# Two expert stages of a four-layer block: normalisation of batches 0 to 6 placed inside the attentions ahead, pairs turned early, gates and first products moved

## The reference, cut to what matters

```python
mod = (_silu(L1_c) @ L1_wmod).reshape(L1_c.shape[0], 6, 1, -1)
sa, ca, ga, sb, cb, gb = (mod[:, 0], mod[:, 1], mod[:, 2], mod[:, 3], mod[:, 4], mod[:, 5])
...
gb = (2 * (gb >= 0) - 1) * jnp.maximum(jnp.abs(gb), 0.25)
...
x = x + ga * _L1_attn_ref(h, ...)
h = _layernorm(x, axis=-1) * (1 + cb) + sb
x = x + gb * _L1_ffn_ref(h, ...)          # top 4 of 32 experts by router logits, and a shared one
```

```python
a = entmax15(layernorm_noaffine(jnp.einsum('btd,de->bte', x, proj)))
g1 = jnp.einsum('bte,er->btr', a, C1)
z = jnp.einsum('btd,dr->btr', xb, Win) * gate     # first product of cp_mumoe
```

## Time and profile before

| | us |
|---|---|
| median of 3 runs | 2562.01 |
| lowest and highest of them | 2559.89, 2563.37 |
| the profiled execution | 2557.01 |
| its span in the trace | 2555.2 |
| layer 1: from the last DVE step of the attention to the logits | 1299.4 to 1344.1 |
| layer 2: from the last row maximum to the first expert product | 1896.9 to 1968.1 |

### The profile page before, as it was taken

How to read it: one execution, slowest core, us unless ns; L and a number is a source line. 1 busy time by engine, 2 the same in 40 slices (tenths; PEclk the granted TensorE clock), 3 DMA queues, 4 the chain that set the end, 5 groups by cost and what they waited for, 6 DMA issues and landing times.

```text
span 2555.2 us, 44079 instructions
## 1 busy us (share of the span) xinstructions
PE 1982.7 (78%) x14690; PEld 1390.1 (54%) x14690; DVE 1679.9 (66%) x5339; ACT 1151.9 (45%) x3371; POOL 894.7 (35%) x1178
## 2 busy tenths in 40 slices
PE   5888889963377667765589999995875799999955
PEld 3545666651266556554575666663443466666642
DVE  6776453245778887888757766665745466666547
ACT  2533333418677777777422222221442355555520
POOL 4433121033456745764440000003410155555511
PEclk7977989975555555555559999996995899999967
DMA  3111000020000000000010000002101000000000
GB/s 124 48 40 40 14 24 27 2 86 23 7 13 7 14 7 14 7 7 1 1 47 1 1 0 0 0 0 46 48 28 63 12 1 1 1 1 1 1 1 17
DMA packets 57812, 49.62 MB, mean 19 GB/s; under 512 B 7049, under 2 KB 55913, under 8 KB 57065
## 3 DMA queue, kind: packets, MB, share of 16 engines
q1 hardware_dynamic: 54548, 45.53, 5.6%
q10 hardware_dynamic: 3040, 1.38, 0.2%
HBM read 19.78 MB, written 1.05 MB: 8 GB/s over the span
## 4 chain that ended last, share of the span: by engine, by line
PE 41%; DVE 28%; SPq 9%; ACT 8%; issue 8%; POOL 5%; DMA 1%; ACTq 0%; DVEq 0%; POOLq 0%
SPq L570 8%; PE bank L1565 5%; PE bank L1557 4%; PE bank L1558 4%; DVE weights L2572 4%; PE bank L1282 3%; PE bank L1634 3%; ACT rope_c L3431 3%; ACT rope_s L3431 3%; PE bank L1671 3%; PE bank L1298 3%; PE bank L1683 2%; DVE small L2610 2%; POOL big L721 2%; DVE feat_o L2622 2%
## 5 line engine op out<-in xcount | busy, mean ns | idle before, releaser
L1468 PE MATMUL bank<-V,probsT 128*128 128x9 f32 x1024 | 236.2, 364 | 76.6 <-ACT probsT L3442 76.6
L1468 PEld LDWEIGHTS bank<-V,probsT 128*128 128x128 f32 x1024 | 226.3, 329 | 114.0 <-ACT probsT L3442 94.4
L2212 DVE TENSOR_REDUCE nmax<-bank 128x4 f32<-128x1024 f32 x144 | 176.0, 1222 | 88.1 <-PE bank L1095 87.9
L3497 ACT ACTIVATE hid<-bank 128x512 f32<-128x512 f32 x144 | 85.6, 597 | 278.1 <-PE bank L1558 268.3
L1565 PEld LDWEIGHTS bank<-weights,hid 128*128 128x128 f32 x1152 | 149.9, 191 | 76.0 <-issue 65.2
L2812 DVE TENSOR_TENSOR hid<-hid,bank 128x512 f32<-128x512 f32 x144 | 98.6, 687 | 117.0 <-PE bank L1565 113.7
L1565 PE MATMUL bank<-weights,hid 128*128 128x128 f32 x1152 | 151.9, 275 | 8.9 <-DVE O L2826 5.1
L3442 ACT ACTIVATE probsT<-bank 128x512 f32<-128x512 f32 x128 | 76.0, 597 | 179.8 <-PE bank L1455 177.4
L1557 PE MATMUL bank<-O,weights 128*128 128x512 f32 x288 | 149.2, 600 | 0.0
L1558 PE MATMUL bank<-O,weights 128*128 128x512 f32 x288 | 147.9, 595 | 0.0
L815 POOL MEMSET big<- 128x4096 bf16 x1 | 3.5, 3511 | 403.6 <-DVE x L2852 403.6
(11 more groups left out here) (664 smaller groups left out, 5502.5 us busy)
## 6 DMA issues: line engine op xcount, KB each, us to landing
qT<-parts SPq DMA_DIRECT2D x276, 32.0 KB
big<-V SPq DMA_DIRECT2D x192, 32.0 KB
big<-parts SPq DMA_DIRECT2D x180, 32.0 KB
weights<-in_weights_l_ffn SPq DMA_DIRECT2D x1, 4832.0 KB, 15.1
weights<-in_weights_l_attn SPq DMA_DIRECT2D x1, 3904.0 KB, 12.6
weights<-in_weights_l_ffn SPq DMA_DIRECT2D x1, 3628.0 KB, 14.3
qT<-V SPq DMA_DIRECT2D x96, 32.0 KB
weights<-in_weights_l_ffn SPq DMA_DIRECT2D x1, 2304.0 KB, 7.9
```

The lines of the kernel that those rows point to most:

```text
L1468: last = mm(pb[1][:, t * S + h * wide:t * S + (h + 1) * wide], probsT[:, h % 2, at:at + P], values_of(b, k)[:, h * wide:(h + 1) * wide], s ...
L2212: V_.tensor_reduce(to, scored.rearrange("p (i a n) -> p i a n", i=HPG, n=n), AX.X, ALU.max, negate=True).then_inc(score_max.sem, 1)
```

## The change

Statistics and normalisation are cut in three groups: batches 0 to 5 (12 tiles), batch 6 (2 tiles), batch 7 (2 tiles), as `FRONT_GROUPS`. Groups 0 and 1 are done inside the attention ahead, group 2 in the front. New helpers `wide_stats_of`, `wide_norm_of` (DVE) and `wide_root` (POOL) do one group each.

```diff
+        FRONT_GROUPS = ((0, B - 2), (B - 2, B - 1), (B - 1, B))
...
+            def wide_root(ph, g):
+                (first, end), (_, _, var_w, rstd_w) = FRONT_GROUPS[g], front_room(ph)
+                at = slice(T * first, T * end)
+                pool.wait_ge(wide_var_ready.sem, wide_var_ready(ph, 0, g + 1))
+                nc.gpsimd.tensor_tensor(rstd_w[:, at], var_w[:, at], minus_half[:, at], ALU.pow).then_inc(wide_rstd_ready.sem, 1)
...
                 for m, there in iterations(ph):
+                    if m in (3 * B - 1, 3 * B):
+                        wide_root("l2_ffn", m - 3 * B + 1)
                     if there(0):
                         split_max(m, 1)
...
+                wide_root("l1_ffn", 0)
+                wide_root("l1_ffn", 1)
                 add_out(B - 1)
...
             def wide_front(ph, logits):
-                pe.wait_ge(pass_done.sem, pass_done(ph, 0, 1))
...
+                for u in range(PAIRS - 1):
+                    turn(u)
                 pe.wait_ge(wide_silu.sem, wide_silu(ph, 0, 1))
                 for b in range(B):
                     last = mm(pb[6 + b // 4][:, b % 4 * D:(b % 4 + 1) * D], silu_8[:, b, :], W(ph, "wmod")[:, 2 * D:3 * D],
                               start=True, stop=True)
                 last.then_inc(wide_mod.sem, 1)
...
+                for u in range(PAIRS - 1):
+                    logits_of(u)
+                turn(PAIRS - 1)
+                logits_of(PAIRS - 1)
...
                 wide_front(ph, "proj")
+                for u in range(PAIRS):
+                    if u == 0:
+                        pe.wait_ge(wide_var_ready.sem, wide_var_ready(ph, 0, 4))
+                    if u == 2:
+                        pe.wait_ge(delta_ready, 1)
+                    mm(pb[RANK_BANKS[u]][0:R2, :], W(ph, "win1"), feats[:, 2 * u:2 * u + 2, :].rearrange("p r k -> p (r k)"),
+                       start=True, stop=True).then_inc(z_psum.sem, 1)
                 pe.wait_ge(mix_ready, 1)
...
                 for m, there in iterations(ph):
                     for k in range(NU):
+                        if m in (3 * B - 1, 3 * B) and k in (0, 3):
+                            (wide_norm_of if k else wide_stats_of)("l2_ffn", m - 3 * B + 1)
...
+                wide_stats_of("l1_ffn", 0)
+                wide_stats_of("l1_ffn", 1)
+                wide_norm_of("l1_ffn", 0)
+                wide_norm_of("l1_ffn", 1)
                 weighed(B - 1)
                 l1_result(B - 1)
...
                 logits = pb[1][:, 0:N16 * E2].rearrange("p (j e) -> p j e", e=E2)
-                wide_gates(ph)
                 dve.wait_ge(wide_logits.sem, wide_logits(ph, 0, 1))
...
                 V_.tensor_scalar(wide_var, one, 1.0 / E2, LN_EPS, ALU.mult, ALU.add).then_inc(wide_var_ready.sem, 1)
-                dve.wait_ge(wide_rstd_ready.sem, wide_rstd_ready(ph, 0, 2))
+                wide_gates(ph)
+                dve.wait_ge(wide_rstd_ready.sem, wide_rstd_ready(ph, 0, 4))
```

More of the change, by code:

```diff
@@ L303, in adaln_program, with normed_of, front_room @@
         shift_8, scale_8 = rows(28, 1)[:, 160:168], rows(28, 1)[:, 168:176]
+        FRONT_GROUPS = ((0, B - 2), (B - 2, B - 1), (B - 1, B))
+        def normed_of(ph):
+            of = rows(8, 8) if ph == "l1_ffn" else hid[:].rearrange("p a c n -> p (a c n)")
+            return of.rearrange("p (j d) -> p j d", d=D)
+        def front_room(ph):
+            room = rows(28, 1) if ph == "l1_ffn" else colmax[:]
+            roots = (room[:, 128:144], room[:, 144:160]) if ph == "l1_ffn" else (best[:], rowsum3[:])
+            return (room[:, 0:6 * N16].rearrange("p (j n) -> p j n", n=6), room[:, 96:128].rearrange("p (j n) -> p j n", n=2), *roots)
         one, total = rows(29, 1)[:, 0:N16], rows(29, 1)[:, N16:2 * N16]
@@ L987, in _ @@
                     continue
-                for n in range(n_wide_norm[ph] if ph != "l3_ffn" else 0):
-                    pool.wait_ge(wide_var_ready.sem, wide_var_ready(ph, 0, n + 1))
+                if ph in ("l1_ffn", "l2_ffn"):
+                    wide_root(ph, 2)
+                if ph == "l2_ffn":
+                    pool.wait_ge(wide_var_ready.sem, wide_var_ready(ph, 0, 4))
                     nc.gpsimd.tensor_tensor(wide_rstd, wide_var, minus_half[:], ALU.pow).then_inc(wide_rstd_ready.sem, 1)
@@ L1016, in wide_front, with turn, logits_of @@
                 last.then_inc(wide_mod.sem, 1)
+                def turn(u):
+                    pe.wait_ge(wide_ready.sem, wide_ready(ph, 0, 1 if u < PAIRS - 1 else 3))
+                    for i in range(4):
+                        last = nc.tensor.transpose(pb[2 + u][:, i * P:(i + 1) * P], normed_of(ph)[:, 4 * u + i, :], C("ident"))
+                    last.then_inc(wide_turned.sem, 1)
+                def logits_of(u):
+                    n = W(ph, logits).shape[1]
+                    pe.wait_ge(wide_feat.sem, wide_feat(ph, 0, u + 1))
+                    for j in range(4 * u, 4 * u + 4):
+                        last = mm(pb[1][:, j * n:(j + 1) * n], feats[:, j // T, j % T * P:(j % T + 1) * P], W(ph, logits),
+                                  start=True, stop=True)
+                    if u == PAIRS - 1:
+                        last.then_inc(wide_logits.sem, 1)
+                for u in range(PAIRS - 1):
+                    turn(u)
                 pe.wait_ge(wide_silu.sem, wide_silu(ph, 0, 1))
@@ L1582, in l2_front @@
                     last.then_inc(mix_turned, 1)
-                for u in range(PAIRS):
-                    mm(pb[RANK_BANKS[u]][0:R2, :], W(ph, "win1"), feats[:, 2 * u:2 * u + 2, :].rearrange("p r k -> p (r k)"),
-                       start=True, stop=True).then_inc(z_psum.sem, 1)
                 for u in range(PAIRS):
@@ L1928, in wide_front @@
                 V_.tensor_scalar(scale_8, pb[0][:, B:2 * B], 1.0, None, ALU.add).then_inc(wide_scaled.sem, 1)
-                dve.wait_ge(wide_rstd_ready.sem, wide_rstd_ready(ph, 0, 1))
-                for j in range(N16):
-                    last = V_.tensor_scalar(normed[:, j, :], x[:, j, :], wide_moments[:, j, 0:1], wide_rstd[:, j:j + 1], ALU.subtract, ALU.mult)
-                    if j % 4 == 3:
-                        last.then_inc(wide_ready.sem, 1)
+                wide_norm_of(ph, 2)
             def wide_gates(ph):
@@ L2737, in l1_front @@
                 take_pair_first(ph)
+                dve.wait_ge(wide_mod.sem, wide_mod(ph, 0, 2))
                 wide_step_of(V_.memset(rows(18, 2), 1.0))
```

32 lines of the change are left out of this document (21 added, 11 removed).

## The result

| | before | changed |
|---|---|---|
| median of the runs, us | 2562.6 | 2544.4 |
| lowest and highest | 2559.9, 2563.4 | 2539.0, 2545.5 |
| profiled execution, its span | 2557.0, 2555.2 | 2544.8, 2542.7 |

The ratio of the two is 0.9932, with a 95% interval from 0.9917 to 0.9947: 17 us faster (14 to 21), against 7 forecast. The range of the prediction ended at 2549.0, 4.6 us above what came.

A forecast was written before the change was run, and what follows sets the result against it. No engine bounds the whole; the chain of waits at the two layers' seams was read. Terms -8.4 + 5.9 + 1.5 - 3.2 - 2.8 = -7.0 took 2562.0 to 2555.0 us, range 2549.0 to 2563.0.

The forecast's parts named there:

- `win1`, turns and `c12`: Layer 2, `win1` off the path from turns to `c12`: -2.8 us, the middle of -1.1 and -4.6.
- Layer 1's early part: Statistics, roots and norms of 14 tiles moved into layer 1's attention fit in DVE's idle time and cost nothing.
- Layer 1's row on PE: Out projection to logits in layer 1: 14.1 us with the clock rising late in the gates, -8.4 us.
- loops of experts that differ in length: Sign that the prediction is wrong: expert loops, whose work is unchanged, differ in length.
- the forecast's own bound: Layer 1's front with the clock rising before the gates: 12.65 us, -9.9 us.
- The stall on POOL: Layer 2's attention: the 12-column root ahead of the last `split_max` delays the cut, +5.9 us, between 5.0 and 6.5.
- hidden after all: Rival: layer 2's root adds no new wait, as other chain work would be late anyway; -14.4 us, 2547.6, chance 0.05.
- Clock behind the stall: Layer 2's attention: PE's clock drops while it stands still; +1.5 us, a quarter of the possible +6.0.
- The rival that ended slower: Rival: clock stays low to the attention's end, +6.0, both fronts low; +5.3 us in all, 2567.3, chance 0.05.
- Layer 2's front: Out projection to entmax in layer 2: logits after 13.6 us, gates behind the variance; -3.2 us.
- with the clock kept to the end, 1.3 more: Layer 2's front if the clock stays high to the end: -4.5 us instead of -3.2.
- clock early and kept: Rival: clock rises early and stays in both fronts, no clock loss behind the stall; -13.1 us, 2548.9, chance 0.15.

The follow-up runs named there:

- `root_behind`: Changed kernel with the POOL roots of layer 2's groups 0 and 1 moved behind `split_max`; 2539.3 us against 2557.0 before, ratio 0.9923.
- `l1_only`: Layer 1's part of the change alone, layer 2's attention and front as in the kernel before; 2550.0 us, ratio 0.9967 to before.
- `pe_wait`: Changed kernel with PE's wait for the finished `x` back at the head of both fronts; ratio 0.9957 to before.
- `filler`: Changed kernel with four unread products of `win1`'s size on PE between `c12` and the expert loop; ratio 0.9941 to before.
- `both_fill2`: Changed kernel with layer 2's roots behind `split_max`, its DVE gates ahead of the logits, two unread products behind `c12`; 2532.6 us, ratio 0.9904 to before.

## Why the prediction was wrong

It named the right stages and mechanisms, and was off in the size of four terms, mostly by the clock: TensorE was at 1.00 earlier in both fronts and in the turns of the mixing weights than its sum had it. By its steps, with the stage table:

| term | forecast | in the traces |
|---|---|---|
| layer 1, up to the logits | -8.4 | -11.57 |
| layer 1, loop of experts | 0 | +1.67 |
| layer 2, stall on POOL | +5.9 | +5.74 |
| clock behind the stall | +1.5 | +0.31 |
| layer 2, front to entmax | -3.2 | -6.41 |
| `win1`, turns and `c12` | -2.8 | -6.31 |
| the rest of the stages | 0 | -0.56 |
| sum | -7.0 | -17.13 |

- **Layer 1's early part: right.** The 12-column root took 2.3 us as read off the line between 16 and 2 columns, all ended by 1314.6, with 7.98 us of DVE's idle time left. It cost nothing.
- **Layer 1's row on PE: too long by 3.1.** The step that failed is "I take the rise where it was, 1328.7 (late in the gates)". That is 7.1 us behind the out projection; it came 3.6 behind it (1329.8), half a microsecond into the gates. The words "the narrow logits did not keep it up" failed too: it stayed up through 24 records of logits, turns and the pause for ACT. Gates took 2.2 instead of 3.35. Not all of it was the clock. "12 turns (0.26 each by 4.20 for 16, 3.15)" took its price from turns that waited for DVE's norms, which took the same 4.20 us; unhindered and still at 0.50, twelve took 2.6 us (1326.68 to 1329.27). And scale and shift began before the out projection had ended, 0.5 us instead of 1.0 behind it. These two make 1.05 of the difference. Of the 11.6 us, 1.7 came back. From the logits to the first expert product behind the choice of experts it is 9.03 us (1337.15 to 1346.18), as before; but then TensorE was at 0.50 from 1346.9 to 1350.2, and the step to the next such product took 4.39 us instead of 2.71. The text had named loops of experts that differ in length as a sign that it is wrong, and this one does. That the layer comes out at -9.9, the forecast's own bound, is luck: -11.6 and +1.7 were both missed.
- **The stall on POOL: right to 0.2 us**, place, cause and size, and `root_behind` removes it. The rival "hidden after all" fell with it.
- **Clock behind the stall: the sign was right, the size was not.** PE was at 0.50 for 5.0 us and the tail behind the cut was 0.3 us longer in all. The rival that ended slower needed 6.0 us from this; it falls. The Trainium skill, "TensorE: Matmul & The Clock Gate", section "HAM oscillation — how this bites in real kernels", has the next burst start cold behind such a gap. By that rule the trace agrees (0.50 behind 6.23 us of standing still). The burst paid little, since PE had waited for ACT in the kernel before, and the slower products filled that wait. PE's timeline, before:

```profile
1901.81 0.40 PE L1116 MATMUL bank<-big 57*128 57x128 bf16 x8 [1.38 <-ACT O L3274]
```

And in the changed kernel, without a wait:

```profile
1901.68 0.61 PE L1148 MATMUL bank<-big 57*128 57x128 bf16 x8
```

- **Layer 2's front: half of the gain was missed.** Its clock rose at 1916.9, ahead of the gates, so that the logits were read 10.6 us behind the out projection and not 13.6: the step "with the rise some 0.9 us before the gates' end" failed, and "with the clock kept to the end, 1.3 more" was no bound, since it began from the late rise. Moreover the front of before was read off one execution in which the logits ran at 1.00 (3.78 us); `l1_only` shows the same code at 6.85. The forecast took its price from one execution; which of the two is the usual one, two profiles do not tell. The other half of the step, that the gates would cost some 2.1 us behind the variance, was right: 1.9.
- **`win1`: outside both bounds.** The step "From the turns on: 3.6 + 7.2 = 10.8 against 11.9, -1.1; or 3.6 + 3.6, -4.6" took the turns at 0.50 in either case. They ran at 1.00 (1.84 us) in seven of the ten profiles with the second pair right ahead of them, and `c12` at 1.00, or nearly, in nine. The bound -4.6 left that out; -6.3 came. Why not in all ten isn't settled: `root_behind`, with the same code there, took 10.7 us, only 1.2 less than before.

The rival with the right mechanism was *clock early and kept*, -13.1: it had 0.15. (*The root is hidden after all*, -14.4, is nearer in number, but its reason fell with the stall.) What came differs from it by the turns at 1.00 and by the rise ahead of the gates in layer 2. Adding the forecast to the median instead of to the profiled execution was right: the same stages differ by up to 5.9 us in the stretch ahead of layer 1's seam and by 3.5 behind layer 2's loop from one execution to the next.

## What to carry to other kernels

A pause that is removed from TensorE's row can be worth more than its length, since the clock may rise earlier (3.0 us for 2.59 and 3.85 for 1.53 in `pe_wait`): bound each such term with every step in it at both levels, also those that ran slowly in the one profile at hand. A row is a price only if the engine did not wait for another inside it, as the turns before did for DVE's norms. Work moved into another engine's idle time must stand behind, not ahead of, whatever that engine's queue still owes the chain: here a root that nobody needed yet stood ahead of a cut that everybody waited for, and cost 6 us. And before a stage of the kernel before is used as a price, look at it in a second execution.

## What the runs showed of the hardware that was not expected

- The clock fell to 0.50 under unbroken work (`filler`, 1954.7), and went on at 0.50 for 12.4 us of fully busy PE in the changed kernel (1955.4 to 1967.8), where the pause ahead was 1.92 us; without the pause, the loop's first products were at 1.00 from the start, or nearly, in `filler` (1959.95) and `both_fill2` (1945.59). Why so long in the one case isn't settled.
- The same code took 3.78 or 6.85 us (layer 2's logits), 3.70 or 7.19 (`c12`), from one execution to another.
- GpSimd's power of 128 x 12 took 2.27 to 2.30 us, 128 x 2 took 0.70 and 128 x 16 took 2.90: a straight line in the columns.
